# A decoder layer on one core: the router reads the residual itself, the last head's sums go straight to the rows that are sent, GpSimd takes a share of the drain, and one move carries two quarters

## The reference

```python
x = x + attn(_layernorm(x), W_qkvb, W_o, ln_g, ln_b)      # fast-weight memory, 16 heads
x = x + xattn(_layernorm(x), ctx, Wq, Wk, Wv, Wout, bout) # cross attention, 8 heads of 128
x = x + ffn(_layernorm(x), router_w, w1, w2)              # 8 experts, one per token

# _L0_ffn_ref, T = 2048 tokens, E = 8 experts, C = 256 places each
logits = x_flat @ router_w
probs = softmax(logits); expert_idx = argmax(probs); gate = probs[expert_idx]
pos = cumsum(onehot(expert_idx)) - 1;  keep = pos < C
expert_in[expert_idx, pos] += x_flat * keep
hidden = gelu(expert_in @ w1);  expert_out = hidden @ w2
y = expert_out[expert_idx, pos] * (gate * keep)
```

## Time and profile before

| | |
|---|---|
| median of 3 runs | 1465.25 us (1464.15 to 1467.24) |
| profiled execution, device time | 1461.66 us |
| its span in the profile | 1459.9 us |
| TensorE clock granted, mean | 0.974 |
| PE / DVE / ACT / POOL busy | 92% / 78% / 64% / 59% |
| first instructions of the drain | about 1274 us from the start of the span |
| last scatter, `ex_xn` load, first expert matmul | 1347.63, 1350.20, 1355.95 us |

### The profile page before, as it was taken

The page is one execution under the profiler, slowest core; times in us unless marked ns, Lnnn a source line. Parts: engine busy times, 40 slices in busy tenths (PEclk is TensorE's granted clock), DMA queues, the critical chain, the costliest instruction groups (busy, mean ns, idle before and its releaser), DMA issues.

```text
span 1459.9 us, 22138 instructions
## 1 busy us (share of the span) xinstructions
PE 1341.5 (92%) x7240; PEld 1095.1 (75%) x7240; DVE 1135.3 (78%) x1748; ACT 935.7 (64%) x1286; POOL 862.3 (59%) x524
## 2 busy tenths in 40 slices
PE   3999999988999899999999999999999999974898
PEld 3778787886788677777777777777777777754898
DVE  6779998958513688898988888898888888977454
ACT  3543434125555587888877878888788878743674
POOL 1400012115412398998988989989889889704353
PEclk9999999999999899999999999999999999986899
DMA  9102024125565677777777877777777777683572
GB/s 274 18 7 66 1 48 105 34 55 201 197 202 186 190 203 187 205 204 191 213 186 192 216 180 208 206 192 207 196 193 207 193 179 206 164 240 146 184 244 88
DMA packets 196542, 241.41 MB, mean 165 GB/s; under 512 B 58595, under 2 KB 101989, under 8 KB 196432
## 3 DMA queue, kind: packets, MB, share of 16 engines
q1 hardware_dynamic: 132128, 143.13, 35.0%
q10 hardware_dynamic: 62256, 91.04, 23.5%
q0 software_dynamic: 2048, 5.90, 1.1%
...
...
## 4 chain that ended last, share of the span: by engine, by line
PE 35%; ACTq 14%; ACT 10%; DVE 8%; issue 5%; POOL 2%; DMA 1%; SPq 1%; DVEq 0%; POOLq 0%
ACTq L997 13%; PE xa_S L1435 13%; PE xa_O L1452 6%; PE xa_Y L1392 5%; ACT xa_probs L1601 5%; ACT xa_pT L1595 4%; PE ex_H L1892 3%; PE ex_Y L1904 3%; PE xa_O L1392 3%; DVE xa_mxp L1218 2%; PE xa_Y L1464 2%; DVE xa_tq L1231 2%; POOL xa_pT L1121 1%; DVE hall L1251 1%; ACTq L1567 1%
## 5 line engine op out<-in xcount | busy, mean ns | idle before, releaser
L1121 POOL TENSOR_TENSOR xa_pT<-xa_moved,xa_pT 128x1024 fp32r<-128x1024 f32 x244 | 581.1, 2402 | 48.0 <-ACT xa_pT L1595 47.1
L1435 PE MATMUL xa_S<-xa_kT,xa_qT 128*128 128x512 f32 x1536 | 399.5, 409 | 34.4 <-ACT xa_probs L1601 32.8
L1452 PE MATMUL xa_O<-xa_pT,xa_v 128*128 128x512 f32 x1536 | 378.3, 395 | 8.4 <-DVE xa_pT L1272 5.5
L1435 PEld LDWEIGHTS xa_S<-xa_kT,xa_qT 128*128 128x128 f32 x1536 | 285.9, 191 | 127.5 <-ACT xa_probs L1601 64.5
L1452 PEld LDWEIGHTS xa_O<-xa_pT,xa_v 128*128 128x128 f32 x1536 | 291.0, 190 | 76.1 <-DVE xa_pT L1272 6.5
L1231 DVE STREAM_TRANSPOSE xa_tq<-xa_probs 128x1024 f32<-128x1024 f32 x256 | 316.8, 1238 | 37.4 <-ACT xa_probs L1601 35.6
L1601 ACT ACTIVATE xa_probs<-xa_S,xa_mxnb 128x1024 f32<-128x1024 f32 x256 | 286.1, 1118 | 71.3 <-DVE xa_mxnb L1221 47.0
L1595 ACT ACTIVATE xa_pT<-xa_moved 128x1024 fp32r<-128x1024 f32 x256 | 269.5, 1060 | 83.0 <-issue 64.7
L1216 DVE TENSOR_REDUCE xa_mxnb<-xa_S 128x1 f32<-128x1024 f32 x128 | 155.8, 1217 | 76.8 <-PE xa_S L1435 75.0
L1218 DVE TENSOR_REDUCE xa_mxp<-xa_S 128x1 f32<-128x1024 f32 x128 | 157.6, 1231 | 20.6 <-PE xa_S L1435 20.6
L467 PE MATMUL fw_pp<-fw_hT,fw_wqk 128*128 128x512 f32 x384 | 100.2, 411 | 9.9 <-DVE fw_F L613 8.4
(11 more groups left out here) (223 smaller groups left out, 1802.7 us busy)
## 6 DMA issues: line engine op xcount, KB each, us to landing
xa_moved<-xa_tq ACTq DMA_DIRECT2D x1024, 64.0 KB, 2.1
xa_moved<-xa_tq SPq DMA_DIRECT2D x1024, 64.0 KB, 2.1
...
ex_w2s<-in_L_ffn_w_dram SPq DMA_DIRECT2D x8, 1024.0 KB, 10.2
```

Of the source, the lines that this page charges most:

```text
L1121: pool.tensor_tensor(quadrants(pT[LO], r), unit_moved(r), quadrants(pT[HI], r).bitcast(F32), ALU.subtract).then_inc(lo_ready, 1)
L1435: last = pe.matmul(S[:, k], qT[a][:, i // GT % 2, q], kT[b][h % 2][:, k * 512:(k + 1) * 512], start=(n == 0), stop=(n == 2))
L1452: last = pe.matmul(O[:], v[a][:, j * P:(j + 1) * P], pT[b][:, r % PRING, k], start=(j == 0 and n == 0), stop=(j == JT - 1 and n == 2))
```

## The change

In words, edit by edit:

1. `add_output` of the last head writes the new residual into the row buffer (`rows[..., X1:]`) instead of `hall`; the copy by ScalarE (`copy_x1`) is gone. The quads 0 and 1 take the upper half of the row buffer, which is free while the last head runs.
2. The router's weights are centred once, early (`share`, `mxp`, one VectorE subtraction), and the router reads the residual itself: transposes, logits and `choose` need no statistics. Only the gate's exponential and the rows that are sent need the root. The exponential is four instructions a quad, each with scale and sum, in place of one and a VectorE sum.
3. The rows are normalised by GpSimd (`scale_rows`, four instructions a quad) for q = 0 to 2, by ScalarE for q = 3.
4. In the drain, p = 122 is GpSimd's; from p = 123 on VectorE makes the even low parts and GpSimd the odd ones.
5. The quarters p = 124 and 125 are moved together: 16 DMAs of 128 KB, all issued by SP (`move_pair`), all counted on one semaphore. ScalarE issues none for them. p = 127 goes to a place of its own (`xa_last`). ScalarE's moves of 126 and 127 stand behind the high parts and copies of their slot.
6. The table `ROUTING` is new; both PSUM halves of a transposed quad are copied by ScalarE. `positions`, `row_logits` and `out_project` of group 30 stand ahead of `weighted` in a slot. GpSimd makes its constants at slot 123. The number of VectorE instructions in `choose` and `place_rows` is smaller.

The core of the diff:

```diff
-        ROUTING = {"root": (0, 2, 6, 9), "rows": (0, 3, 6, 9), "transposes": (1, 4, 7, 10), ...
+        OUTPUTS = {(30, 0): 3, (30, 1): 3, (31, 0): 7, (31, 1): 7}
+        SUMS = {(30, 0): 3, (30, 1): 4, (31, 0): 7, (31, 1): 7}
+        ROUTING = {"transposes": (0, 2, 5, 8), "copies": (0, 2, 5, 8), "logits": (1, 3, 6, 9), "choose": (2, 4, 6, 9),
+                   "positions": (3, 5, 7, 10), "place": (4, 6, 8, 11),
+                   "statistics": (None, None, 5, 8), "root": (2, 2, 5, 8), "scale": (2, 3, 5, 9), "rows": (3, 4, 6, 9),
+                   "exp": (4, 4, 6, 10)}
...
-        LAST = SLOTS - LAG + 1
+        LAST = SLOTS - LAG + 2
...
+        def move_pair(eng, p, a, b):
+
+            g, q = divmod(p, GT)
+            keys = slice(q * JT // GT, (q + 2) * JT // GT)
+            eng.dma_start(moved[32 * b:32 * b + 32, p % MRING:p % MRING + 2, a].rearrange("p r j n -> p r (j n)"),
+                          tq[32 * a:32 * a + 32, g % 2, b, keys].rearrange("p (r j) m n -> p r (j m n)", r=2)) \
+                .then_inc(arrived[g // 8][q], 16)
...
+                if p == SLOTS - 3:
+                    continue
                 sp.wait_ge(tr_done, 2 * (GT * g + GT - 1) + q // 2 + 1)
-                if p >= MRING:
-                    sp.wait_ge(lo_ready, 2 * (p - MRING) + 2)
+                if p == SLOTS - 4:
+                    low_until(sp, 2 * (p - MRING) + 3)
+                    for d in range(4):
+                        for a in (0, 2, 1, 3):
+                            move_pair(sp, p, a, a ^ d)
+                    continue
...
+            def scale_rows(q):
+
+                pool.wait_ge(rstd_rows, q + 1)
+                for i in range(4 * q, 4 * q + 4):
+                    last = pool.tensor_scalar(rows[:, place_of(i), 0:D], rows[:, place_of(i), X1:X1 + D], rs[:, i, 0:1],
+                                              rrstd[:, i:i + 1], ALU.subtract, ALU.mult)
+                last.then_inc(scaled, 1)
...
-                if p >= 0:
+                if 0 <= p < LAST:
                     low_part(2 * p)
                     low_part(2 * p + 1)
+                elif LAST <= p < SLOTS:
+                    low_part(2 * p + 1)
...
+            dve.wait_ge(pj_mm, KU + 1)
+            dve.tensor_tensor(rw[:], rw[:], mxp[:, 0:E].unsqueeze(1).to_broadcast([P, DC, E]), ALU.subtract)
...
-                    last = dve.scalar_tensor_tensor(hall[:, FLAT[i + m]], Y[k][:, m], rinv[:, inv][:, m:m + 1],
+                    dst = rows[:, place_of(i + m), X1:X1 + D] if g // 4 == XH - 1 else hall[:, FLAT[i + m]]
+                    last = dve.scalar_tensor_tensor(dst, Y[k][:, m], rinv[:, inv][:, m:m + 1],
                                                     hall[:, FLAT[i + m]], ALU.mult, ALU.add)
...
             def row_exp(q):
                 act.wait_ge(shifted, q + 1)
-                act.activation(four(ex[:], q), four(ex[:], q), ACT.Exp).then_inc(expd, 1)
+                act.wait_ge(rstd_rows, q + 1)
+                for i in range(4 * q, 4 * q + 4):
+                    last = act.activation(spent[:, i], ex[:, i], ACT.Exp, scale=rrstd[:, i:i + 1], accum_out=gate[:, i:i + 1])
+                last.then_inc(expd, 1)
...
+                issued = 0 <= m < SLOTS and m not in (SLOTS - 4, SLOTS - 3)
```

More of the change, by code:

```diff
@@ new lines, in constants @@
+            def constants():
+                pool.wait_ge(chunk_lo, len(order))
+                pool.memset(ones[:], 1.0).then_inc(consts, 1)
+                pool.wait_ge(consts, 1)
+                pool.affine_select(out=before[:], in_=ones[:], compare_op=ALU.is_gt, fill=0.0, base=0,
+                                   pattern=[[1, P]], channel_multiplier=-1).then_inc(consts, 1)
+                for e in range(E):
+                    last = pool.memset(rank[:, e:e + 1], float(E - e))
+                last.then_inc(consts, 1)
+                pool.iota(token[:], pattern=[[P, TILES]], base=0, channel_multiplier=1).then_inc(consts, 1)
@@ L1124, in _ @@
+            def scale_rows(q):
[4 more added lines that the diff above has]
+                last.then_inc(scaled, 1)
             for c in chunks_of(-1):
                 chunk_low(c)
[L1126 removed]
+            for s in range(END):
@@ L1150, in _ @@
+                if s < SLOTS:
+                    for c in chunks_of(s):
+                        chunk_low(c)
+                if s == SLOTS - 5:
+                    constants()
+                for q in due("rows", s):
+                    if q < QUADS - 1:
+                        scale_rows(q)
             for q in range(QUADS):
@@ L1320, in choose @@
+                then(dve.tensor_tensor(oh[:, quad(q)], oh[:, quad(q)], wide(top[:, quad(q)]), ALU.is_equal))
+                for n in range(4 * q + 1, 4 * q + 4):
+                    then(dve.tensor_tensor(pre[:, n], pre[:, n - 1], oh[:, n - 1], ALU.add))
                 dve.sem_inc(oh_ready, 1)
+                dve.tensor_scalar(limit[:, quad(q)], top[:, quad(q)], -float(CAP), float((E + 1) * CAP), ALU.mult, ALU.add)
+                dve.tensor_copy(rows[:, quad_rows(q), TOKEN], token[:, quad(q)])
@@ L1406, in _ @@
             pe.wait_ge(w_hi, 4)
+            pe.wait_ge(rw_in, 16)
+            for c in range(DC):
+                pe.matmul(mxp[:, 0:E], share[:], rw[:, c], start=(c == 0), stop=(c == DC - 1))
             for n in range(VU):
```

337 lines of the change are left out of this document (169 added, 168 removed).

## The result

The changed kernel took 1473.81 us in the median of 9 runs (1469.97 to 1478.54); the kernel before, run beside it, 1466.61 (1462.00 to 1469.73). The ratio is 1.0058, 95% interval 1.0040 to 1.0076: slower by more than the 0.2% that count as a difference. The forecast was 1470.5 in 1461.5 to 1479. The profiled execution took 1474.51 us, span 1472.8.

The account below looks back on a forecast made before the run. Waits between engines in drain and routing bound the kernel, GpSimd's last scatter ending last. Later scatters (+3.3 us) and collisions (2.0) made +5.3: 1467.0 for the profiled execution, 1470.5 for the median, range 1461.5 to 1479.

Parts of the forecast that it names:

- collisions: Drain, VectorE's small steps held under GpSimd's low parts and scalings: 0 to 9 us, 2.0 taken.
- Double moves: Drain, SP's sixteen 128 KB moves of 124 and 125: issued from 1279.8, all in at 1291.9.
- ScalarE: Drain: behind those moves, two high parts, a copy, eight moves of 126, table load and root in order, until 1301.0.
- TensorE's gap as the largest shift: Drain: TensorE idle some 18 us, then at the low clock; `weighted(124)` ends at 1315.5, before at 1300.2.
- The second half of the path: Drain after `weighted(124)`: ScalarE's first high part of 127 ends 1322.0, VectorE's quad 2 Newton step 1327.0, scatters start 1330.0.
- The rival in which the lock decides: `choose(0)` on VectorE falls under GpSimd's low part of 125 and scaling of quad 0: +12.3 us, 1477.5; chance 0.15.
- The scaling of quad 2: GpSimd's four scalings just ahead of the scatters: 3.0 us taken, lower end 1.5.
- The stream: GpSimd's sixteen scatters in one run: 20.2 us plus 1.7 for stretching by VectorE's splits, ending 1351.9, +3.3 us.
- Costed at nothing: Centring (0.5 us if not hidden), constants (1 us if uncovered), `copy_x1`, shorter `place` and `choose`, main-loop waits: nothing added.

Follow-up runs that it names:

- the second ones: Changed kernel and kernel before, each profiled once more unchanged: last exponential to last scatter 81.24 and 74.82 us; ratios to the kernel before 1.0062 and 1.0008.
- experiment 5: Changed kernel with units 124 and 125 moved by eight plain moves each from SP and ScalarE; last exponential to last scatter 83.93 us, ratio to kernel before 1.0056.
- 6: Changed kernel with `choose(0)` one slot earlier on VectorE; last exponential to last scatter 75.33 us, ratio to kernel before 1.0015.
- experiment 7: Changed kernel with VectorE making both low parts of units 123 to 127, GpSimd none; last exponential to last scatter 80.27 us, ratio to kernel before 1.0066.
- experiment 1: Changed kernel with ScalarE instead of GpSimd scaling quads 0 to 2; last exponential to last scatter 80.13 us, ratio to kernel before 1.0045.

## Why the prediction was right

Right in sign and place, and near in size: +5.3 us forecast, 7.2 between the first profiles (6.4 between the second ones). Some of the agreement is luck, since errors cancelled; they are named below. By its steps, the forecast's times counted from 1273.75, the measured ones from the last exponential:

| step | forecast | measured |
|---|---|---|
| first high part of 124 | 18.2 | 18.1 |
| copy of group 30's sum | 27.5 | 24.8 |
| `choose(0)` done and positions started (forecast without a collision) | 30.6 | 29.9 |
| `weighted(124)` done | 41.8 | 41.2 |
| second high part of 126 done | 43.0 | 42.3 |
| Newton step of quad 2 done | 53.3 | 53.8 |
| scatters start | 56.3 | 58.9 |
| last scatter ends (with 2.0 for collisions) | 80.2 | 82.05, 81.24 |

- *Double moves*: right to 0.1 us in time, and experiment 5 gives their price on the path, 1.3 to 1.4 us.
- *ScalarE*: 2.7 us too late. I set the eight issues behind the activations; they ran beside them, only the table load waited for issues. The collision at `choose(0)` took 2.0 of it back.
- *TensorE's gap as the largest shift*: confirmed by 6, which takes 5.9 to 6.7 us back. The run behind it came out right by luck: I took the logits at the low clock (3.6, measured 3.56) but `out_project` at its full-clock price, 2.0, and it took 3.76; `weighted(124)` was put at 4.6, and its last matmuls were fast, so it took 3.3.
- *The second half of the path*: the right time by another route. I let it run over the exponentials, the high and low part of 127 and the statistics of quad 2. Without the hold the statistics would have been done at 1330.15. What `ex_shift` waited for was the table load behind the copies of quad 2's transposes, done at 1331.72, and with it `weighted(126)` and its clock.
- *Collisions, 2.0 taken*: 2.0 in the timeline at `choose(0)`, 1.8 by experiment 7, and perhaps as much again at `choose(1)`. The rival in which the lock decides was at work at its place, by one low part and not by the scaling behind it.
- *The scaling of quad 2, 3.0 us*: this is the term that was mis-sized. It took 4.83. I had drawn a line through two shapes of a two-input subtraction and read 0.74 us for 256 elements; the scaling, another instruction with one tensor input, took 1.21. I also left out that the scaling of quad 1, 5.23, stands between the low parts of 126 and 127; by experiment 1 `weighted(127)` didn't wait for it.
- *The stream*: 22.4 to 23.1 us instead of 21.9; the two stretched scatters cost 2.0 to 2.8, not 1.7.
- *Missed as a mechanism*: in the changed drain the clock can fall again behind a wait of only 2.12 us. The forecast had no term for it; a `weighted(126)` at the low clock costs 3.2 us more, and one of three profiles of that program up to there has it.
- *Costed at nothing*: what lies outside the drain isn't settled. The differences of the medians exceed those of the measure by 2.1 us in the mean of the twelve changed forms; the kernel before against itself shows 1.5. No profile shows a place for it, and no run took the centring alone.
